# Pairwise bilinear products on one core: x kept in four tiles' room, loaded two tiles at a time beside the stores

## The reference

```python
vid = jnp.einsum('bfd,de->bfe', x, W)
idx_i, idx_j = jnp.triu_indices(F_, k=1)
return x[:, idx_i, :] * vid[:, idx_j, :]
```

## Time and profile before

| What | Value |
|---|---|
| median of three runs | 1284.27 us |
| profiled execution: span from its first to its last instruction | 1282.9 us |
| the median less that span | 1.4 us |
| moved by DMA | 553.70 MB in 11810 packets |
| HBM read, written | 33.59 MB, 520.09 MB |
| VectorE busy | 1079.9 us (84%) in 273 instructions |
| TensorE busy (matmul) | 184.4 us (14%) |

### The profile page before, as it was taken

The page is one execution under the profiler, slowest core; times in us unless marked ns, Lnnn a source line. Parts: engine busy times, 40 slices in busy tenths (PEclk is TensorE's granted clock), DMA queues, the critical chain, the costliest instruction groups (busy, mean ns, idle before and its releaser), DMA issues. The chain is left out here.

```text
span 1282.9 us, 1255 instructions
## 1 busy us (share of the span) xinstructions
PE 184.4 (14%) x256; PEld 71.9 (6%) x256; DVE 1079.9 (84%) x273; POOL 0.2 (0%) x4
## 2 busy tenths in 40 slices
PE   2012110302111030300020211103020030202100
PEld 1000000100000010100010000001010010100000
DVE  6589989988897989998028989989998899899980
POOL 0000000000000000000000000000000000000000
PEclk7555565655655565655565565656565565655655
DMA  9999999999999999999999999999999999999999
GB/s 406 424 427 438 435 433 435 443 431 427 437 438 433 425 437 434 436 429 445 418 419 427 436 430 436 438 438 424 440 439 429 432 435 439 425 439 439 431 423 409
DMA packets 11810, 553.70 MB, mean 432 GB/s; under 512 B 1312, under 2 KB 1312, under 8 KB 1312
## 3 DMA queue, kind: packets, MB, share of 16 engines
q1 hardware_dynamic: 6048, 277.38, 50.1%
q10 hardware_dynamic: 5760, 276.30, 49.9%
HBM read 33.59 MB, written 520.09 MB: 432 GB/s over the span
## 5 line engine op out<-in xcount | busy, mean ns | idle before, releaser
L295 DVE TENSOR_TENSOR mem<-mem,vid 128x1024 f32<-128x1024 f32 (+11 forms) x270 | 1079.3, 4065 | 161.5 <-DMA out_dram<-mem 113.2
L315 PE MATMUL vid<-mem,w 128*128 x256 | 184.4, 888 | 1010.2 <-PEq L313 1010.2
L315 PEld LDWEIGHTS vid<-mem,w 128*128 128x128 f32 x256 | 71.9, 295 | 1121.9 <-issue 1121.9
L226 DVE COPY w<-mem 64x64 f32<-64x64 f32 x2 | 0.4, 189 | 5.0 <-DMA mem<-in_r_x_dram 4.9
L223 DVE MEMSET w<- 128x128 f32 x1 | 0.2, 165 | 0.8 <-PEq L340 0.8
L340 POOL MEMSET const-bfloat16-1.0<- 128x1 bf16 x1 | 0.1, 102 | 0.0
L340 POOL MEMSET const-uint8-127<- 128x1 uint8 x1 | 0.1, 102 | 0.0
L340 POOL MEMSET const-float32-0.0<- 128x1 f32 x1 | 0.1, 98 | 0.2 <-issue 0.2
L340 POOL MEMSET const-float32-1.0<- 128x1 f32 x1 | 0.1, 98 | 0.0
## 6 DMA issues: line engine op xcount, KB each, us to landing
out_dram<-mem SPq DMA_DIRECT2D x9, 7680.0 KB, 23.3
out_dram<-mem ACTq DMA_DIRECT2D x3, 7680.0 KB, 23.1
out_dram<-mem SPq DMA_DIRECT2D x3, 7168.0 KB, 21.6
out_dram<-mem ACTq DMA_DIRECT2D x3, 5120.0 KB, 17.5
out_dram<-mem ACTq DMA_DIRECT2D x2, 7168.0 KB, 22.6
out_dram<-mem ACTq DMA_DIRECT2D x2, 6656.0 KB, 21.4
out_dram<-mem SPq DMA_DIRECT2D x2, 6656.0 KB, 19.8
out_dram<-mem ACTq DMA_DIRECT2D x3, 4096.0 KB, 17.5
```

What stands on the lines that cost most here:

```text
L226: lambda: nc.vector.tensor_copy(w2[half, half], mem[half, place + F, :D]),
L295: lambda: nc.vector.tensor_tensor(o, left, right, ALU.mult),
L315: last = nc.tensor.matmul(vid[:, b : b + BANK, :], lhsT=w2[:, :], rhs=xt(b), start=True, stop=True)
```

## The change

From tile 4 on, x has units 0 to 127 and no more: the places of four tiles. Tiles 4 to 7 stand there already, from the first group. Then `LOADS` has four transfers of two tiles each, issued at the start of tiles 6, 8, 10 and 12 for tiles 8, 10, 12 and 14 and the tiles after each. Each goes into the 64 units that the two tiles before last have left, and waits for their products. The transfers at tiles 6 and 8 are issued on SP's queue, while the stores are on ACT's; those at 10 and 12 on ACT's, while the stores are on SP's (`TURN`: from slot 45 on). No store waits for a load any more except the first one of the program. PE's loop is cut at tiles 8 and 12 (`RUNS`), without a wait of its own; the product that raises `free` waits for the next tile's load at every tile.

The slots are the same up to slot 23. From slot 24 (in tile 4) they are 106, 106 and 105 pairs at units 128, 234 and 340, over and over to the end of tile 12; then x gives up units, and the slots are 117, 116, 116 twice, three of 127 and four of 102. There are 76 slots instead of 74. The host lays x out in the order of the new transfers.

```diff
-GROUPS = [
-    (0, [(96, 224), (26, 96), (0, 26)]),
-    (8, [(154, 256), (26, 154), (0, 26)]),
-]
-STRETCHES = [37]
+LOADS = [
+    (0, (96, 224), 1),
+    (0, (26, 96), 1),
+    (0, (0, 26), 1),
+    (6, (64, 128), 8),
+    (8, (0, 64), 10),
+    (10, (64, 128), 12),
+    (12, (0, 64), 14),
+]
+RUNS = [0, 8, 12]
+TURN = 45
...
-    (104, 208, 64), (128, 312), (128, 112), (128, 240, 72), (128, 96), (128, 224, 16), (112, 80), (120, 192, 32),
+    (106, 128), (106, 234), (105, 340), (106, 128), (106, 234), (105, 340), (106, 128), (106, 234),
...
-    first = max(begin for begin, _ in GROUPS if begin <= t)
-    return TOP - (t - first + 1) * fields
+    first = max(begin for begin in RUNS if begin <= t)
+    return (TOP if first == 0 else TOP // 2) - (t - first + 1) * fields
...
-    def load(g):
-        (begin, pieces), end = GROUPS[g], ends(NT)[g]
-        begin = max(begin, 1)
-        low = place_of(end - 1, F)
+    order = order_of(NT)
+
+    def load(trigger):
         sems = []
-        for lo, hi in pieces:
-            at = (begin - 1) * F + lo - low
-            sems.append(transfer(mem[:, lo:hi, :], x[:, at : at + hi - lo, :], (lo, hi), False, after((lo, hi)), act if g else sp))
-            loads.append((range(begin, end), (lo, hi), sems[-1]))
+        for when, (lo, hi), begin in LOADS:
+            if when == trigger:
+                later = [b for _, _, b in LOADS if b > begin] + [NT]
+                tiles = range(begin, min(later))
+                low = place_of(tiles[-1], F)
+                at = order.index(tiles[-1]) * F + lo - low
+                queue = act if when >= begins[1] + 2 else sp
+                sems.append(transfer(mem[:, lo:hi, :], x[:, at : at + hi - lo, :], (lo, hi), False, after((lo, hi)), queue))
+                loads.append((tiles, (lo, hi), sems[-1]))
         return sems
...
-        transfer(rows[:, : end - begin, :], mem[:, units[0] : units[1], :], units, True, needs, act if slot < STRETCHES[0] else sp)
+        transfer(rows[:, : end - begin, :], mem[:, units[0] : units[1], :], units, True, needs, act if slot < TURN else sp)
...
-        if t in begins[1:]:
-            hold = load(begins.index(t))
-            for late in held:
-                store(*late)
-            held = []
+        if t:
+            load(t)
...
-            if tells is free and t + 1 < NT and t + 1 not in begins:
+            if tells is free and t + 1 < NT:
                 needs += loaded(t + 1)
...
-        if begin:
-            for s, n in pe.waits(loaded(begin)):
-                nc.tensor.wait_ge(s, n)
```

More of the change, by code:

```diff
@@ L154, in place_of, with order_of @@
 def place_of(t, fields):
-    first = max(begin for begin, _ in GROUPS if begin <= t)
-    return TOP - (t - first + 1) * fields
+    first = max(begin for begin in RUNS if begin <= t)
+    return (TOP if first == 0 else TOP // 2) - (t - first + 1) * fields
 def ends(tiles):
-    return [begin for begin, _ in GROUPS[1:]] + [tiles]
+    return RUNS[1:] + [tiles]
+def order_of(tiles):
+    begins = sorted({begin for _, _, begin in LOADS})
+    return [t for begin, end in zip(begins, begins[1:] + [tiles]) for t in range(end - 1, begin - 1, -1)]
 def overlap(a, b):
@@ L248, in loaded @@
         return [(sem, 16) for tiles, piece, sem in loads if t in tiles and overlap(piece, units)]
+    begins = RUNS
     hold = load(0)
-    begins = [begin for begin, _ in GROUPS]
-    held = []
     def store(slot, last):
@@ L301, in pairwise_bilinear_kernel @@
             if at == end:
[L302 to L307, removed]
+                store(slot, counts[made])
     for sem, n in sp.waits([(sem, 16) for _, _, sem in moved]):
@@ L316, in half @@
         last.then_inc(there, 1)
-    pe = Queue(nc.tensor, behind)
     for begin, end in zip(begins, ends(NT)):
-        if begin:
-            for s, n in pe.waits(loaded(begin)):
-                nc.tensor.wait_ge(s, n)
         base = place_of(begin, F)
@@ L348 @@
     x0[:, F, :D] = _np.concatenate([w, w])
-    x = x[:, [t for (begin, _), end in zip(GROUPS, ends(NT)) for t in range(end - 1, max(begin, 1) - 1, -1)]]
+    x = x[:, order_of(NT)]
     x = _np.pad(x.reshape(2 * D, (NT - 1) * F, C), ((0, 0), (0, PAD), (0, 0)))
```

## The result

The changed kernel took 1293.4 us (median of 5 runs, 1291.9 to 1295.2), the kernel before 1284.27 beside it: 1.0069 times as long, 95% interval 1.0057 to 1.0082. It is slower by 9.1 us, where 4.4 were forecast; the sign was right and the size was half. The time lies in the range of 1282 to 1312, but above the 1287 to 1292 that the forecast gave for its own case. The profiled execution has a span of 1292.4 us, 9.5 above that of before.

A forecast was written before the change was run, and what follows sets the result against it. DMA transfers were taken as the bound, at 2.310 us per MB. Span 1282.9 - 1.4 (middle load's edges) + 0.2 (more transfers) + 4 x 1.4 (loads among stores) = 1287.3, as median 1288.7 us; range 1282 to 1312.

The forecast's parts named there:

- its own case: Four loads starting among running stores, each one entry and one exit: 1287 to 1292 us, chance 0.42.
- The table of slots: New store slots, in rounds of three: about 13 us spare each round, so costed at nothing.
- VectorE's 18.09 and 41.40 us waits: VectorE's idle times around the middle load at tile 8: they go, worth nothing to the end.
- the edges of the middle load: Load-only stretch around 640 to 680 us removed: saves its entry and exit, 1.1 + 0.3 = 1.4 us.
- 4 x 1.4 = 5.6: Four loads starting while stores run, at about 450, 610, 770 and 930 us: 1.4 us added each.
- The failed step: alternation: At each load among stores, an engine's share moves as one block: one entry and one exit, 1.4 us.
- Rival 2: At the four loads, load and store rows alternate, 0.3 to 1.4 us a row: 1293, 1309 or 1328 us; chance 0.19.
- the entry forecast at about 1.1 us: Stores giving way to a load, at each of four loads: about 1.1 us lost; each exit 0 to 1.1.
- The sum: Whole kernel, from the profiled span: 1282.9 - 1.4 + 0.2 + 4 x 1.4 = 1287.3 us; as median 1288.7.
- rival 4: Stream runs dry in rounds of three slots or at tile 4.7's slot change: one 3 us gap, 1292 us; chance 0.04.
- Hidden edges: At the four loads, entries between two queues cost nothing: 1283.1 us, up to 1286.8; chance 0.30.
- overlap: Engines load and store at once, so 39 us of loading is partly free: 1283 down to 1244 us; chance 0.05.

The follow-up runs named there:

- the move in the kernel before: Kernel before the change, with its second group of loads on SP's queue instead of ACT's, starting beside the last store of the first half: 1285.43 us, 1.001.

## Why the prediction was right in sign and half in size

**What held.** The transfers are the bound, the bytes didn't change, and each kernel's time is bytes at 2.310 us per MB plus losses. The table of slots was costed at nothing, and with the turn it costs at most 1.2 us (the run without loads). VectorE's 18.09 and 41.40 us waits went and were worth only the edges of the middle load. Four loads beside stores lose 5.7 us of packet time where 4 x 1.4 = 5.6 were forecast; that the two agree so well is luck, since the same four lose 4.0 us without a turn.

**The failed step: alternation.** I costed a load at one entry and one exit because I took an engine's share of a transfer to move as a block, from the earlier trace rows. The trace of the changed kernel shows the opposite. One engine's packets during the first load (which packets are one engine's is inferred: each starts 0.004 us before the one before ends, as among stores alone):

```
start us   queue  bytes   took us
481.073    ACT    53760   1.985   store row
483.054    SP     32768   1.213   load row
484.263    ACT    53760   1.985
486.244    SP     32768   1.213
487.454    ACT    53760   1.985
```

Rival 2's mechanism is what happens, row by row; its prices were wrong. Each row takes what its bytes cost (53,760 B on each of 16 engines is 0.86 MB, 1.99 us), and a change of queue and direction between two rows leaves no time at all, where the rival put 0.3 to 1.4 us. What the loads lose lies elsewhere. In the four stretches 204 of some 1500 rows took 0.05 to 2.4 us longer than most rows of their size, and these make nearly all of the 5.7 us. At the first and the third load most of that (1.0 and 1.7 us of the mean) lies in the rows that start around the load's beginning; at the second and the fourth more than half (0.65 and 0.62) lies in mid-load, around the place where one store gives way to the next (651 to 657 and 977 to 982 us). So the entry forecast at about 1.1 us came to 1.0 and 1.7 at two loads and to 0.3 and 0.2 at the others, the exits to 0.1 or less, and the picture of blocks was wrong.

, on which I had rested it, could hardly tell. The store issued at 38.34 us had its first row at 41.61, 3.3 us later; the changed kernel's loads had theirs 3.0 to 5.0 us after their issue (471.37 to 476.38 us at the first, 797.93 to 800.92 at the third). So the 18 packets from 40.7 to 41.6 us started before a row of the store could be expected, and of the 28 behind them 16 were small ones and 12 rows, at most two on an engine. The Trainium skill (DMA: Bandwidth & Descriptors, section on queues, rings and completion order) says that an engine takes turns between queues with work, a packet at a time, and that it drains a packet of typically 9 to 17 descriptors before it switches. The turn-taking agrees; the size doesn't, if a row is one descriptor: 8 rows and a small packet would go as one piece, and here one row does.

**The missing term: the slowest engine.** The sum counted mean losses. But an engine moves its own rows of every transfer and none of another's, so nothing hands an engine's lag to the others while all are busy, and the kernel ends with the last one. The rows that took longer fell on the engines unequally: during the first load they cost one engine 0.25 us and another 3.13. Before, the ends of a transfer's 16 shares stayed 0.7 to 1.8 us apart all along. After, they were 1.04 us apart ahead of the first load, 2.65 behind it, 5.13 behind the second, 6.58 behind the fourth. This term is 4.3 us of the 9.5, and the sum has nothing for it. That it comes with the loads is shown by leaving them out (1.20 us), and that it goes by their number by the eight loads (10.35 us, +4.1 at the end); with the loads in the stores' queue it is 3.01 and 3.24 us. It is not a fixed price on top of the rest: with the turn at 54 or 66 the ends are only 2.1 us apart, and those kernels are no faster than the one without a turn (1289.59 and 1288.87 against 1288.93), because the middle holds more.

**The gap (rival 4).** The stream did run dry once, not in the rounds of slots, where I looked, but at the turn from ACT's queue to SP's. Slot 44, the last on ACT, and slot 45, the first on SP, share the engines; slot 44 was 47.3 us from issue to landing, where stores of its size there take 33 to 35:

```profile
out_dram<-mem ACTq DMA_DIRECT2D x1, 6720.0 KB, 47.3
```

VectorE waited the 15.45 us for its room, slot 47 was issued at 783.74 us, and its first packets began at about 784.6. The eleven engines that were ahead had finished slot 46 by 781.9 to 782.4 us and were idle for 2.2 to 2.8 us. The wait alone makes no gap: three kernels with the same turn have it too, 15.4 us long, and no gap (the loads in the stores' queue; no loads; turn at 45 with all loads on SP). Their engines were 1.0 to 2.4 us apart at the turn, those of the two executions of the changed kernel 5.1 and 5.0. The later turns fit: 4.51 us and a gap of 1.3 on the mean at slot 54, 2.94 and 0.06 at slot 66. That the spread is the condition is inferred from these seven traces; it was not set by itself.

**The rivals' other claims.** Hidden edges are refuted by the move in the kernel before (+1.2 us, not a gain), overlap by a price that never fell below 2.31 us per MB with both queues at work.

**Open.** Why the third load costs 1.7 to 2.0 us right behind the gap but next to nothing with stores in ACT's queue throughout (785 to 835 us: 50.0 us for bytes worth 49.8), and why single loads lie anywhere between 0.1 and 2.7. The loads right behind a gap cost 1.7 to 2.0 us in all three executions that have one; that the gap, by putting the engines more nearly in step, makes the next load dear fits them but was not tested by itself. Also open: why a spread sometimes narrows, as in the kernel before with its load moved; why the spread behind the second load differs from kernel to kernel with the same transfers up to there (2.35 us in one, 5.0 and 5.1 in two); and which engines fall behind, and why. Times with loads beside stores also scatter more (1287.3 to 1292.7 in one kernel) than those of before (1283.7 to 1285.9), which fits a spread that comes out differently each time, but wasn't tested. None of the versions beat the kernel before; the nearest with four loads is 1287.08 us.

## What to carry to other kernels

Where the DMA engines are the bound and always busy, the time is that of the slowest engine, so beside the mean loss of a disturbance ask how unequal it leaves the engines, and read it from the small packets that end the last transfer. If loads must go among stores, try the stores' own queue: that was 1.9 us better here than beside them in another queue when the stores kept one queue, and 4.9 to 6.0 when they changed theirs between the loads. Few and large loads were better than many small ones (6.1 us, shown for loads beside the stores only). And a stretch of loads alone can be cheaper than it looks: the one of before, with VectorE idle for 41 us, lost 1.4 us.

## What the runs showed of the hardware that was not expected

- Two queues with work on one engine take turns row by row, whatever the direction, and a change leaves no time between the rows (481 to 489 us, above). What a load beside stores costs lies in some 50 rows of each stretch that took up to 2.4 us longer than others of their size.
- A queue that joins while an engine is busy has its first row 3.0 to 5.0 us after the issue (four loads of the changed kernel); on idle engines it took 0.8 (slot 47).
- A lag between engines can stay as it is while all are busy (6.58 us at every store from 997 us to the end, in the changed kernel), or narrow slowly (from 2.92 to 1.43 us in some 510 us, in the kernel before with its load moved). Eight loads of 32 places beside the stores left the 16 engines 10.35 us apart at the end, four of 64 places 5.25, none 1.20.
- A change of the stores' queue delays the last store of the old queue (47.3 us to landing instead of 33 to 35), while its rows and those of the new queue's first store alternate.
